# Third-period windows gathered by GpSimd, and half of the second residual stage moved into the last pair of the fourth period

## The reference, cut to what matters

```python
x = x + _L0_gnn_ref(relu_layernorm(x), adj, ...)
x = x + _L1_gnn_ref(relu_layernorm(x), adj, ...)
x = x + _L2_gnn_ref(relu_layernorm(x), adj, ...)   # this layer
x = x + _L3_gnn_ref(relu_layernorm(x), W, adj)

def _L2_gnn_ref(x, adj, Wg0, bg0, Wg1, bg1, Wih, Whh, bih, bhh):
    h = relu(einsum('ts,bsh->bth', adj, x @ Wg0 + bg0))
    h = relu(einsum('ts,bsh->bth', adj, h @ Wg1 + bg1))
    for p in range(1, 5):                 # the four periods
        nw = 128 // p                     # windows of p nodes
        wins = h[:, :nw * p, :].reshape(B * nw, p, H)
        last = _lstm_last(Wih[p-1], Whh[p-1], bih[p-1], bhh[p-1], wins)
        h = h.at[:, arange(nw) * p + (p - 1), :].set(last)
    return h
```

## Time and profile before

| | |
|---|---|
| median of 3 runs | 1432.02 us (1428.77 to 1432.37) |
| the profiled execution, its own time | 1430.7 us |
| its span, first to last instruction | 1429.0 us |
| mean granted TensorE clock | 0.946 of full |
| PE busy | 1043.3 us, 73% of the span |
| DVE busy | 975.4 us, 68% |
| ACT busy | 735.8 us, 51% |
| POOL busy | 335.4 us, 23% |
| chain that ended last | PE 56%, DVE 26%, issue 8%, ACT 5% |

### The profile page before, as it was taken

The page is one execution under the profiler, slowest core; times in us unless marked ns, Lnnn a source line. Parts: engine busy times, 40 slices in busy tenths (PEclk is TensorE's granted clock), DMA queues, the critical chain, the costliest instruction groups (busy, mean ns, idle before and its releaser), DMA issues.

```text
span 1429.0 us, 22097 instructions
## 1 busy us (share of the span) xinstructions
PE 1043.3 (73%) x5403; PEld 638.0 (45%) x5403; DVE 975.4 (68%) x3979; ACT 735.8 (51%) x2053; POOL 335.4 (23%) x1131
## 2 busy tenths in 40 slices
PE   3666666666543241288878688999999999599997
PEld 1444444444422121155543565444455444466665
DVE  7777888888779999955767643544343453768786
ACT  2333344444333336144656575956454554477775
POOL 4044555666437563000100100000020030100000
PEclk9999999999999996599989799999999999599999
DMA  5000000000010000000000000000000000001011
GB/s 151 1 1 0 1 1 2 1 2 1 13 42 1 0 1 1 1 0 0 0 0 0 1 0 0 0 0 0 1 0 0 0 1 0 0 9 30 22 29 31
DMA packets 16659, 12.34 MB, mean 9 GB/s; under 512 B 666, under 2 KB 14531, under 8 KB 16579
## 3 DMA queue, kind: packets, MB, share of 16 engines
q1 hardware_dynamic: 16578, 11.49, 2.9%
HBM read 7.23 MB, written 4.19 MB: 8 GB/s over the span
## 4 chain that ended last, share of the span: by engine, by line
PE 56%; DVE 26%; issue 8%; ACT 5%; POOL 2%; DMA 1%; DVEq 1%; ACTq 0%; POOLq 0%
PE P L1427 32%; PE P L714 13%; DVE arena L369 2%; DVE bst_all L931 2%; DVE arena L489 2%; PE P L1570 2%; ACT hb L1213 1%; DVE arena L494 1%; DVE arena L487 1%; DVE bcol L388 1%; PE P L1563 1%; PE P L1576 1%; PE P L1541 1%; PE P L1559 1%; DVE scal L357 1%
## 5 line engine op out<-in xcount | busy, mean ns | idle before, releaser
L1427 PE MATMUL P<-arena,WT 128*128 (+2 forms) x792 | 330.5, 581 | 3.9 <-ACT L1316 2.9
L1427 PEld LDWEIGHTS P<-arena,WT 128*128 128x128 f32 x792 | 152.4, 193 | 182.0 <-issue 168.2
L1329 ACT ACTIVATE arena<-P,bl 128x512 f32<-128x512 f32 (+1 forms) x252 | 153.8, 637 | 140.3 <-PE P L1427 132.9
L714 PE MATMUL P<-arena 1*128 1x127 f32 (+62 forms) x504 | 150.6, 428 | 89.2 <-DVE arena L369 87.0
L714 PEld LDWEIGHTS P<-arena 1*128 1x128 f32 x504 | 122.1, 308 | 130.9 <-DVE arena L366 120.4
L653 ACT ACTIVATE arena<-arena 1x127 f32<-1x127 f32 (+62 forms) x126 | 32.3, 257 | 165.1 <-DVE arena L380 154.8
L1126 DVE TENSOR_TENSOR arena<-arena 128x512 f32<-128x512 f32 (+1 forms) x36 | 22.0, 611 | 137.6 <-ACT arena L1329 137.6
L1213 ACT ACTIVATE hb<-xN,nmr,rsd 128x128 f32 (+1 forms) x192 | 78.6, 484 | 42.6 <-PE P L1427 30.6
L920 POOL COPY arena<-arena 128x512 f32<-128x512 f32 x16 | 21.2, 1373 | 324.6 <-DVE arena L1137 232.8
L201 POOL TENSOR_SCALAR lf<-lf 1x1 f32<-1x1 f32 x210 | 88.2, 420 | 21.8
L714 PE MATMUL P<-arena,Ib 128*128 128x46 bf16 (+1 forms) x318 | 35.5, 273 | 63.8 <-ACT arena L683 63.1
(11 more groups left out here) (500 smaller groups left out, 2558.9 us busy)
## 6 DMA issues: line engine op xcount, KB each, us to landing
out_dram<-xN SPq DMA_DIRECT2D x16, 256.0 KB, 2.3
Wn<-in_L_gnn_Wih_dram SPq DMA_DIRECT2D x4, 256.0 KB, 2.7
Wn<-in_L_gnn_Whh_dram SPq DMA_DIRECT2D x4, 256.0 KB, 2.6
Wqkv<-in_L_gnn_W_dram SPq DMA_DIRECT2D x1, 192.0 KB
W1n<-in_L_gnn_W_dram SPq DMA_DIRECT2D x1, 128.0 KB
W2n<-in_L_gnn_W_dram SPq DMA_DIRECT2D x1, 128.0 KB
Wg<-in_L_gnn_Wg_dram SPq DMA_DIRECT2D x2, 64.0 KB
adj<-in_adj_dram SPq DMA_DIRECT2D x1, 64.0 KB, 1.8
```

The costliest lines, as they stand in the source:

```text
L714: def mm(o,l,r,start=True,stop=True): return t.matmul(o,lhsT=l,rhs=r,start=start,stop=stop)
L1329: act(s.gt[u][gate][:,0:cols],P[4*u+gate][:,0:cols],f,bias=s.bl[:,4*(p-1)+gate:4*(p-1)+gate+1]).then_inc(ev('lstm_gates'),1)
L1427: def mm(o,l,r,start=True,stop=True,**k): return t.matmul(o,lhsT=l,rhs=r,start=start,stop=stop,**k)
```

## The change

GpSimd also gathers the windows of the third period (24 copies of 336 columns before the 16 of 512), into the same eight buffers, and the copies of a step's windows wait for the multiplication of the same step one pair earlier; PE reads contiguous buffers in periods 3 and 4. The two pairs of the fourth period are written out (no hardware loop) on PE and DVE, and in the second, in each step and for each u, PE transposes one group of `R2` (groups 0 to 7, whose LSTM results are complete after the first pair) into bank `P[4*u+3]` before it multiplies gate 3 there; DVE adds it to x and takes its statistics. PE transposes straight out of `R2`, for the later groups too, so ACT's 16 copies into `zb` go. The residual stage behind the LSTM does groups 8 to 15.

```diff
@@ -912,12 +912,15 @@ def gpsimd_windows(s,eng):
-    for g in range(4):
-        it,u=g//2,g%2
-        eng.wait_ge(ev('lstm_hidden'),32+6*g+6+2)
-        if it: eng.wait_ge(ev('lstm_gate_sums'),s.gates_before(4,it-1,3,u)+4)
-        for st in range(4):
-            eng.tensor_copy(s.lw[u][st].rearrange("p (b w) -> p b w",w=32),s.win(g,4,st)).then_inc(ev('lstm_windows'),1)
+    for p,pairs in ((3,4),(4,2)):
+        _,nw,cols,_=s.lstm_shape(p)
+        for it in range(pairs):
+            for st in range(p):
+                for u in range(2):
+                    if st==0: eng.wait_ge(ev('lstm_hidden'),s.hidden_before(p,it,u))
+                    read=(p,it-1) if it else (3,3)
+                    if it or (p==4 and st<3): eng.wait_ge(ev('lstm_gate_sums'),s.gates_before(*read,st,u)+(4 if st else 3))
+                    eng.tensor_copy(s.lw[u][st][:,0:cols].rearrange("p (b w) -> p b w",w=nw),s.win(2*it+u,p,st)).then_inc(ev('lstm_windows'),1)
@@ -1110,34 +1113,49 @@ def vector(s,v,c):
     v.sem_inc(ev('lstm_hidden'),2)
+    v.sem_inc(ev('residual_x'),2)
+    def early_residual(p,it,st,u):
+        if p<4 or it==0: return
+        tt(X(2*st+u),X(2*st+u),P[4*u+3][:,:],ALU.add).then_inc(ev('residual_x'),1)
+        v.wait_ge(ev('residual_x'),NG+2+2*st+u+3)
+        s.ln_stats(v,xN,2*st+u)
+    def lstm_pair(p,base,it):
+        _,nw,cols,_=s.lstm_shape(p)
+        early=p==4 and it==1
+        if early:
+            v.wait_ge(ev('residual_product'),NG+2+3)
+            early_residual(p,it,0,0)
+        for st in range(p):
+            if early:
+                v.wait_ge(ev('residual_product'),NG+2+2*st+4)
+                early_residual(p,it,st,1)
...
+            for u in range(2):
...
+                if early and u==0 and st<3:
+                    v.wait_ge(ev('residual_product'),NG+2+2*st+5)
+                    early_residual(p,it,st+1,0)
...
-    with v.Fori(0,NP-1) as it:
+    with v.Fori(NP//2,NP-1) as it:
         for u in range(2): residual(NG+2,it,u)
         for u in range(2): residual_stats(NG+2,it,u)
@@ -1185,6 +1203,13 @@
+  def lstm_pairs(s,eng,p,body):
+    pairs=s.lstm_shape(p)[3]//2
+    if p==4:
+        for it in range(pairs): body(it)
+    else:
+        with eng.Fori(0,pairs) as it: body(it)
@@ -1333,11 +1359,6 @@ def scalar_main(s,a):
-    a.wait_ge(ev('lstm_hidden'),base+2)
-    with a.Fori(0,NP) as it:
-        for u in range(2):
-            a.wait_ge(ev('residual_product'),NG+2+2*it+u+1)
-            act(s.zb[u][:,:],R2[:,bass.ds((2*it+u)*C,C)],ACT.Copy).then_inc(ev('residual_mixed'),1)
@@ -1485,35 +1506,41 @@ def tensor(s,t):
+    t.sem_inc(ev('residual_product'),2)
+    def to_rows(out,g):
+        for b in range(GB): i=t.transpose(out[:,b*N:(b+1)*N],s.R2[:,bass.ds(g*C+b*N,N)],I[:,:])
+        i.then_inc(ev('residual_product'),1)
...
                 t.wait_ge(ev('lstm_gates'),s.gates_before(p,it,st,u)+6-s.gates_kept(st,u))
-                if p==4: t.wait_ge(ev('lstm_windows'),4*(2*it+u)+st+1)
+                if early:
+                    t.wait_ge(ev('lstm_hidden'),base+8+1+(st>1))
+                    to_rows(P[4*u+3],2*st+u)
+                if p>2: t.wait_ge(ev('lstm_windows'),(24 if p==4 else 0)+2*p*it+2*st+u+1)
                 elif p>1 and st==0: t.wait_ge(ev('lstm_hidden'),s.hidden_before(p,it,u))
-                xs=s.lw[u][st][:,:] if p==4 else s.win(2*it+u,p,st)
+                xs=s.lw[u][st][:,0:cols] if p>2 else s.win(2*it+u,p,st)
                 for gate in gates:
+                    if early and gate==3: t.wait_ge(ev('residual_x'),NG+2+2*st+u+3)
...
     t.wait_ge(ev('lstm_hidden'),base+2)
-    with t.Fori(0,NP) as it:
-        for u in range(2):
-            g=2*it+u
-            t.wait_ge(ev('residual_mixed'),NG+2*it+u+1)
+    for it in range(NP//2,NP):
+        for u in range(2):
             t.wait_ge(ev('residual_x'),NG+2+2*it+u+1)
-            for b in range(GB): i=t.transpose(P[6+u][:,b*N:(b+1)*N],s.zb[u][:,b*N:(b+1)*N],I[:,:])
-            i.then_inc(ev('residual_product'),1)
+            to_rows(P[6+u],2*it+u)
```

More of the change, by code:

```diff
@@ L1112, in vector @@
     v.sem_inc(ev('lstm_hidden'),2)
+    v.sem_inc(ev('residual_x'),2)
[15 more added lines that the diff above has]
+            for u in range(2):
+                gi,gf,gg,go=(t[:,0:cols] for t in s.gt[u])
+                cbu=s.cb[u][:,0:cols]
+                before=s.gates_before(p,it,st,u)
+                v.wait_ge(ev('lstm_gates'),before+(6+2))
+                if st==0: tt(cbu,gi,gg,ALU.mult).then_inc(ev('lstm_cell'),1)
+                else:
+                    tt(gi,gi,gg,ALU.mult).then_inc(ev('lstm_cell_parts'),1)
+                    v.wait_ge(ev('lstm_gates'),before+(6+3))
+                    tt(cbu,cbu,gf,ALU.mult).then_inc(ev('lstm_cell_parts'),1)
+                    v.wait_ge(ev('lstm_cell_parts'),s.igb[p]+4*(it*(p-1)+st-1)+2*u+2)
+                    tt(cbu,cbu,gi,ALU.add).then_inc(ev('lstm_cell'),1)
+            for u in range(2):
+                k=base+2*(it*p+st)+u+1
+                go=s.gt[u][3][:,0:cols]
+                tc=s.tcb[u][:,0:cols]
+                v.wait_ge(ev('lstm_tanh_cell'),k)
+                if st<p-1: tt(s.hp[u][:,0:cols],go,tc,ALU.mult).then_inc(ev('lstm_hidden'),1)
+                else: tt(s.win(2*it+u,p,st),go.rearrange("p (b w) -> p b w",w=nw),tc.rearrange("p (b w) -> p b w",w=nw),ALU.mult).then_inc(ev('lstm_hidden'),1)
+                if early and u==0 and st<3:
+                    v.wait_ge(ev('residual_product'),NG+2+2*st+5)
+                    early_residual(p,it,st+1,0)
@@ L1487, in tensor, with lstm_pair @@
     t.wait_ge(ev('conv_out'),NG+2)
+    t.sem_inc(ev('residual_product'),2)
+    def to_rows(out,g):
+        for b in range(GB): i=t.transpose(out[:,b*N:(b+1)*N],s.R2[:,bass.ds(g*C+b*N,N)],I[:,:])
+        i.then_inc(ev('residual_product'),1)
+    def lstm_pair(p,base,it):
+        _,nw,cols,_=s.lstm_shape(p)
+        early=p==4 and it==1
+        for st in range(p):
+            for u in range(2):
+                k=base+2*(it*p+st)+u+1
+                gates=(0,2,1,3) if st else (0,2,3)
+                t.wait_ge(ev('lstm_gates'),s.gates_before(p,it,st,u)+6-s.gates_kept(st,u))
+                if early:
+                    t.wait_ge(ev('lstm_hidden'),base+8+1+(st>1))
+                    to_rows(P[4*u+3],2*st+u)
+                if p>2: t.wait_ge(ev('lstm_windows'),(24 if p==4 else 0)+2*p*it+2*st+u+1)
+                elif p>1 and st==0: t.wait_ge(ev('lstm_hidden'),s.hidden_before(p,it,u))
+                xs=s.lw[u][st][:,0:cols] if p>2 else s.win(2*it+u,p,st)
+                for gate in gates:
+                    if early and gate==3: t.wait_ge(ev('residual_x'),NG+2+2*st+u+3)
+                    out=P[4*u+gate][:,0:cols] if p>2 else P[4*u+gate][:,0:cols].rearrange("p (b w) -> p b w",w=nw)
+                    i=mm(out,s.WT[:,(2*(p-1))*4+gate,:],xs,stop=(st==0))
+                    if st==0: i.then_inc(ev('lstm_gate_sums'),1)
+                if st:
+                    t.wait_ge(ev('lstm_hidden'),k)
+                    for gate in gates: mm(P[4*u+gate][:,0:cols],s.WT[:,(2*(p-1)+1)*4+gate,:],s.hp[u][:,0:cols],start=False).then_inc(ev('lstm_gate_sums'),1)
@@ L1488, in tensor @@
     base=0
     for p in range(1,5):
-        BG,nw,cols,NGp=s.lstm_shape(p)
-        with t.Fori(0,NGp//2) as it:
-            for st in range(p):
-                for u in range(2):
-                    k=base+2*(it*p+st)+u+1
-                    gates=(0,2,1,3) if st else (0,2,3)
-                    t.wait_ge(ev('lstm_gates'),s.gates_before(p,it,st,u)+6-s.gates_kept(st,u))
-                    if p==4: t.wait_ge(ev('lstm_windows'),4*(2*it+u)+st+1)
-                    elif p>1 and st==0: t.wait_ge(ev('lstm_hidden'),s.hidden_before(p,it,u))
-                    xs=s.lw[u][st][:,:] if p==4 else s.win(2*it+u,p,st)
-                    for gate in gates:
-                        out=P[4*u+gate][:,0:cols] if p==4 else P[4*u+gate][:,0:cols].rearrange("p (b w) -> p b w",w=nw)
-                        i=mm(out,s.WT[:,(2*(p-1))*4+gate,:],xs,stop=(st==0))
-                        if st==0: i.then_inc(ev('lstm_gate_sums'),1)
-                    if st:
-                        t.wait_ge(ev('lstm_hidden'),k)
-                        for gate in gates: mm(P[4*u+gate][:,0:cols],s.WT[:,(2*(p-1)+1)*4+gate,:],s.hp[u][:,0:cols],start=False).then_inc(ev('lstm_gate_sums'),1)
```

34 lines of the change are left out of this document (7 added, 27 removed).

## The result

The changed kernel takes **1398.62 us**, median of 4 runs (1398.42 to 1399.28), against 1431.10 (1428.77 to 1432.37, 4 runs) of the kernel before: ratio 0.978, 95% interval 0.977 to 0.979. The profiled executions took 1398.59 and 1430.7 us, with spans of 1396.9 and 1429.0: 32.1 us less, where 26.2 was forecast.

The account below looks back on a forecast made before the run. PE's work bounds the kernel up to 1216 us, DVE's the residual stage after it. Terms -29.0 + 4.4 + 0.5 + 0 + 3.0 + 3.0 + 4.0 - 12.1 = -26.2 give 1404.5, or 1405.8 beside the median; forecast 1402 to 1409, wider range 1397 to 1417.

Parts of the forecast that it names:

- Pitch: Third period: gathered contiguous columns shorten PE's input products from 0.45 or 0.44 to 0.2825 us a record, -29.0 us.
- Stalls: Third period: shorter products give less cover, so PE waits within and between pairs, 4 x 1.1 = +4.4 us.
- The rival with copies on the path: GpSimd's copies block DVE on the recurrence's path, 21.8 us in place of 4.4, 1423 us; 1409 to 1424 had chance 0.22.
- Six early copies: Second period, behind its first pair: the first six copies for the third period cost PE +0.5 us.
- 1.02 us moved between boundaries: PE's 1.02 us behind four copies leaves the fourth period's pair boundary and returns between third and fourth periods: 0.
- The new wait: Fourth period, second pair: PE's first transposes wait for u=0's last hidden state, +3.0 us with one copy collision.
- The clock: Fourth period, second pair: after the idle time PE's granted clock falls to half for 6.1 us, +3.0 us.
- Transposes: Fourth period, second pair: 32 transposes on PE in eight groups of 0.5 us, +4.0 us.
- Residual stage: Behind the LSTM: GpSimd starts after two passes instead of six, and the first addition comes earlier without ACT's copy, -12.1 us.
- Nothing for the start: From the start to the LSTM's first marked hidden-state write: forecast change 0.
- My rival of few collisions and no fall of the clock: Stalls 1.4 us, no clock price, 3.5 for transposes, nothing in the second period: 1399 us; 1397 to 1402 had chance 0.16.
- Half clock through the second pair: Fourth period, second pair: PE stays at half clock throughout, 45.4 us in place of 3.0, 1448 us; chance 0.03.

Follow-up runs that it names:

- the kernel that reads neighbouring columns: Changed kernel, but the third period's input products read 336 neighbouring (wrong) columns of `R2` and GpSimd copies nothing for that period; 1396.87 us, ratio 0.977.
- the kernel with the delay alone: Changed kernel, but GpSimd's copies that follow a pair's last products wait for that pair's last hidden states; 1398.28 us, ratio 0.978.
- the first attempt: Changed kernel, but in the fourth period's second pair, first step, each member's transposes move behind gates 0 and 2, before its gate 3; 1396.84 us, ratio 0.978.
- the kernel with the early part alone: Changed kernel with early residual work, but the third period read from `R2` with a stride of three, only the fourth gathered; 1425.8 us, ratio 0.997.

## Why the prediction held, and where it missed

Right in direction and mechanism, 5.9 us too cautious in the profiled execution. The median of 1398.62 lies in the range of 1397 to 1417, near its lower end, and not in 1402 to 1409, which had a chance of 0.50. Nearly every size that was off was off to the same side. Term by term:

- **Pitch, -29.0**: right. Four pairs of 76 records at 0.2825 us are 85.9, and the third period is 3.0 above that; before it was 114.9. Shown by the kernel that reads neighbouring columns.
- **Stalls, +4.4**: 3.0 between the marks, of which 0.7 is the last mark's slip; by PE's own products 2.3, most of it the stops between pairs, 0.25 to 0.37 us idle each and 0.27 for the last record's end. The mis-sized step took two collisions a pair, a certain one of 0.54 us and a race. The certain one measured 0.35, and in the pairs shown the copy lost the race. Collisions were not rare: a copy met the add of either member in every step after a first one, 16 times in the third period and 6 in the fourth's first pair, most of them under cover. The rival with copies on the path is out: the third period's cost 1.0 us in all. The Trainium skill's rule that it names (SBUF — State Buffer, Who interferes with whom), that the two lock each other out, agrees with the trace: all 22 of these adds ended 0.36 to 0.38 us (336 columns) or 0.55 us (512) after the end of the copy that they met, whether the copy had 0.47 us left or 0.95. The size of 0.54 was too large because it scaled the copy's columns, while what counts is how much of the copy is left when the add starts.
- **Six early copies, +0.5**: nothing; the second period repeats to 0.02 us, with these copies and without.
- **1.02 us moved between boundaries, 0**: between the fourth period's pairs it went, as forecast (47.0 to 45.9 in the kernel with the gather alone). At the start of the fourth period about half of it came back: PE idles 0.22 us there and its first pair takes 0.5 us more. Between the marks the first pair is 1.2 us better than I had it, since before only its second mark slipped (L1130 at 1.51 us) and now both do.
- **The new wait, +3.0**: 3.25, with the one collision that I had put in. Its base was read too short: L1137's first write at 1217.18 lasted 1.08 us, not 0.69 (the two take 1.99), so the stop before was 2.5 us and not 2.1. The kernel with the delay alone shows this base, 2.50, and the collision adds 0.75.
- **The clock, +3.0**: 1.7 where it fell. I took the length from a restart that stayed at half for 6.1 us; here it was 3.4. That stretch lay ahead of the LSTM, in work of another kind, and was the wrong row. That it falls at all was no certainty either: after stops of 3.24 and 3.25 us it fell in four traces and not in a fifth.
- **Transposes, +4.0**: 3.4, near my lower end; it is what is left of 8.4 us after the stop and the clock. PE waited nowhere in this pair for DVE's additions, as I had it.
- **Residual stage, -12.1**: 12.3, of which 0.5 is no more certain than the clock: the changed kernel's second trace has 9.4 us there instead of 8.9. How much of it is ACT's copy stays open.
- **Nothing for the start**: 0.8 us of the result is its scatter, which is no work of the change.

My rival of few collisions and no fall of the clock, at 1399, came out at the right number, and that is luck: its stalls were 1.4 us for 3.0 (or 2.3), its clock price nothing for 1.7, and 0.8 of scatter and 1.2 at a boundary, which it did not have, made up for them. Half clock through the second pair did not occur: with a transpose group in every step the clock was back after 3.4 us.

## What to carry to other kernels

When a faster stage shrinks the cover between dependent steps, work out the new cover against the chain behind it, as was done here with 2.26 against 1.70 us: it told that the stalls would be small, and they were 2 to 3 of 29 us. A wait moved to the front of an in-order queue costs its whole length and perhaps a spell of clock; put independent work of the same queue ahead of it, but then look at who frees the bank behind it, since the first attempt only traded 3.25 us of one wait for 3.07 of three. And where a kernel's start scatters by 3 us, compare stages between marks: where the clock does the same they repeat to about 0.1 us and tell apart what ten runs can't. Put a mark on the engine that sets the pace, though; one on another engine can slip by 0.8 us of its own.

## What the runs showed of the hardware

- A matmul's column step matters unevenly: 336 f32 columns took 0.2825 us a record when adjacent, 0.01 more with a step of two, 0.45 with a step of three.
- A GpSimd copy beside DVE's add of two SBUF inputs lengthened it from 0.51 to 0.86 us, and one of 512 columns from 0.69 to 1.48, in the changed kernel, and the copy stretched from 0.63 to 1.01 us beside the DVE instruction in front. The add was held for what was left of the copy: its end came 0.36 to 0.38 us (336 columns) or 0.55 us (512) after the copy's in all 22 cases of the changed kernel's trace.
- The length of PE's stop did not decide whether the granted clock fell from 1.00 to 0.50. It fell after 3.24 or 3.25 us in four traces (two of them of the changed kernel), and after 1.49 with 0.37; it held after 3.24 us, 2.50, 1.49 with 0.80, and 0.70 with 0.37. What decides is open.
- The clock also rose while PE made nothing but transposes. In the residual stage of the kernel with the early part alone (columns as above):

```profile
1226.00:1227.00 1.00, 1.00 (x6) 0.50 0.00 0
1227.00:1228.00 1.00, 0.96 (x5) 0.50 0.00 0
1228.00:1229.00 1.00, 1.00 (x6) 0.50 0.03 8
1229.00:1230.00 1.00, 0.15 (x1) 0.87 0.00 0
1230.00:1231.00 1.00, 0.65 (x5) 1.00 0.00 0
```

The Trainium skill (TensorE: Matmul & The Clock Gate, Part 4: PE-mode transpose) says that transposes do not raise the clock as other matmuls do; here it rose behind 16 of them with no product between, and so it did in the kernel with neighbouring columns (0.50 through 1198, 1.00 from 1200 to 1202), where it fell again over the next ones. In the kernel before it stayed at 0.50 under all 64, as the page has it. So the rule held in one kernel and not in the others; what made the difference is open.
